# Output projection as three rounded products by half blocks, with the weights' parts reloaded through one buffer

## The reference, cut to what matters

```python
x = x + attention(layernorm(x), Wq, Wk, Wv, Wo, betas)
x = x + ffn(layernorm(x), ...)          # gate: top 4 of 32 experts; shared expert beside it
# attention: 16 heads of 128, segments of 64 tokens, a memory carried from segment to segment
att_dot = softmax(q @ k.T / scale, causal) @ v
att_mem = sigma_q @ mem / (sigma_q @ z)
mem    += sigma_k.T @ (v - sigma_k @ mem / (sigma_k @ z))
att     = beta * att_mem + (1 - beta) * att_dot
out     = att.reshape(Bsz, SEG, H * DV) @ Wo      # 2048 x 256: this product is what changes
```

## Time and profile before

| | |
|---|---|
| time, median of 3 runs | 1655.94 us |
| the profiled execution's own time | 1656.93 us |
| its span | 1655.1 us |
| PE busy | 1626.1 us (98%) |
| PE weight loads | 1421.5 us (86%) |
| DVE busy | 1138.9 us (69%) |
| ACT busy | 884.3 us (53%) |
| POOL busy | 495.9 us (30%) |
| DMA moved | 122.07 MB, 74 GB/s on average |
| PE in the chain that ended last | 92% of the span |

### The profile page before, as it was taken

One profiled execution on the slowest core, in us unless ns is written; L12 is line 12 of the kernel. 1 busy time (PEld: TensorE's weight loads), 2 busy tenths in 40 slices (PEclk: granted clock), 3 DMA queues, 4 the chain that ended last, 5 costly groups with the idle time before them and its releaser, 6 DMA issues.

```text
span 1655.1 us, 42788 instructions
## 1 busy us (share of the span) xinstructions
PE 1626.1 (98%) x17260; PEld 1421.5 (86%) x17260; DVE 1138.9 (69%) x3509; ACT 884.3 (53%) x1955; POOL 495.9 (30%) x438
## 2 busy tenths in 40 slices
PE   8899999999999999999999999999999999999898
PEld 7798999899998999898999989898999989986555
DVE  7865857585775757575776758575876767589544
ACT  6564646465563646365664646364654646462131
POOL 2332323232332313331333313231333323230361
PEclk9999999999999999999999999999999999999999
DMA  6102121211102121312112020312112020327957
GB/s 208 27 21 78 40 73 33 81 33 55 58 29 84 36 72 34 86 34 58 49 35 85 29 78 28 86 34 65 42 41 78 29 78 23 95 90 214 315 103 216
DMA packets 121781, 122.07 MB, mean 74 GB/s; under 512 B 24032, under 2 KB 101296, under 8 KB 121456
## 3 DMA queue, kind: packets, MB, share of 16 engines
q1 hardware_dynamic: 118224, 113.52, 23.0%
q0 software_dynamic: 3328, 5.81, 1.8%
q10 hardware_dynamic: 32, 0.01, 0.0%
HBM read 94.90 MB, written 24.40 MB: 72 GB/s over the span
## 4 chain that ended last, share of the span: by engine, by line
PE 92%; DVE 5%; DMA 1%; issue 1%; ACT 0%; POOL 0%; SPq 0%; DVEq 0%; POOLq 0%; ACTq 0%
PE bank_p L1502 23%; PE bank_v L1620 13%; PE chain_k L1575 6%; PE chain_k L1553 6%; PE bank_a L1510 5%; PE bank_v L1510 5%; PE chain_q L1553 5%; PE bank_s L1523 4%; PE bank_a L1591 3%; PE chain L1553 3%; PE bank_p L1533 3%; PE bank_a L1602 2%; PE bank_v L1602 2%; PE bank_s L1608 2%; PE chain L1575 2%; PE bank_p L1683 1%
## 5 line engine op out<-in xcount | busy, mean ns | idle before, releaser
L595 POOL TENSOR_TENSOR step_place<-step_place 128x512 f32<-128x512 f32 x128 | 166.0, 1297 | 574.9 <-ACT step_place L741 426.3
L763 ACT ACTIVATE step_place<-chain_q,step_place 128x128 f32<-128x128 f32 x384 | 112.8, 367 | 221.1 <-DVE step_place L999 221.1
L1620 PE MATMUL bank_v<-step_place 128*128 128x256 f32 x1024 | 225.3, 381 | 0.7 <-ACT step_place L774 0.7
L1502 PE MATMUL bank_p<-xt_hi,w_hi 128*128 128x256 f32 x1024 | 220.0, 296 | 3.0 <-DVE step_place L987 2.9
L1620 PEld LDWEIGHTS bank_v<-step_place 128*128 128x128 f32 x1024 | 193.2, 190 | 29.2 <-issue 2.6
L1502 PE MATMUL bank_p<-xt_hi,w_lo 128*128 128x256 f32 x1024 | 206.4, 283 | 0.0
L1502 PE MATMUL bank_p<-xt_lo,w_hi 128*128 128x256 f32 x1024 | 206.3, 283 | 0.0
L632 POOL TENSOR_TENSOR step_place<-step_place 128x512 f32<-128x512 f32 x64 | 69.3, 1082 | 435.4 <-DVE step_place L1267 435.4
L1502 PEld LDWEIGHTS bank_p<-xt_hi,w_hi 128*128 128x128 f32 x1024 | 158.3, 191 | 22.4 <-issue 13.8
L987 DVE SCALAR_TENSOR_TENSOR step_place<-step_place,bank_p 128x512 f32<-128x512 f32 x128 | 87.4, 684 | 107.6 <-ACT bank_p L735 107.6
L1502 PEld LDWEIGHTS bank_p<-xt_hi,w_lo 128*128 128x128 f32 x1024 | 159.8, 192 | 0.0
(11 more groups left out here) (225 smaller groups left out, 3959.9 us busy)
## 6 DMA issues: line engine op xcount, KB each, us to landing
step_place<-in_L_attn_Wo_dram SPq DMA_DIRECT2D x128, 256.0 KB, 2.8
step_place<-beta_all SPq DMA_DIRECT2D x64, 256.0 KB, 3.3
expert_place<-in_L_ffn_w_dram SPq DMA_DIRECT2D x24, 512.0 KB, 8.2
expert_sums<-zero SPq DMA_DIRECT2D x16, 272.0 KB, 5.2
expert_rows<-rows_place SPq DMA_DIRECT2D x15, 288.0 KB, 2.3
step_place<-in_L_attn_x_dram SPq DMA_DIRECT2D x16, 256.0 KB, 3.9
turned<-in_L_attn_x_dram SPq DMA_DIRECT2D x16, 256.0 KB, 3.9
x_rows<-rows_place SPq DMA_DIRECT2D x16, 256.0 KB, 2.9
```

The lines of the kernel that those rows point to most:

```text
L595: nc.gpsimd.tensor_tensor(dl[seg][:, :, 0:DK], val[:, seg, :, :], beta_rows[:, :, :], ALU.mult).then_inc(s["vb_ready"], 1)
L763: ins = nc.scalar.activation(to[:, j, :], t[:, at:at + DK], ACT.Copy, scale=rd[:, seg, r:r + 1])
L1502: ins = mm(out, w[:, g, m, c, col], x[:, c, :, :].rearrange("p s t -> p (s t)"), start=i == 0, stop=i == len(parts) - 1)
L1620: ins = mm(bank_v[:, b * D:(b + 1) * D], att[:, b * PIECES + i, :], wo[:, i % WR, :], start=(i == 0 and b == 0), stop=(i == PIECES - 1), s ...
```

## The change

- **Format.** `project_out(k)` now makes three fp32r products for each piece: `att_hi` by both parts of `Wo`, `att_lo` by the rounded part. A call does a quarter of a half block: `WR = 4` pieces, 12 products of 128 by 256. A half is 128 rows: both sequences, both segments, half of each segment's tokens. There are `SLOTS` = 128 calls (before: 16 calls of 64 records).
- **Place.** Two calls a step: `project_out(2n - 5)` between the two halves of the keys' projection, `project_out(2n - 4)` before `project_v(0)`. Call 123 and the four calls of the last half block come after the loop.
- **Parts of `Wo`.** At the start `Wo` is loaded whole, split (`wo_high` on ACT, `wo_low` on POOL), and its parts are stored to DRAM (`store_wo`, SP). In the loop POOL loads 1 MB, the four pieces' parts, before each call (`load_wo(k)`, 128 loads). The buffer `wo` holds exactly those four pieces, so load `k` waits for `wo_used` of call `k - 1`.
- **Parts of the attended block.** ACT makes two copies for each segment instead of one (`att_hi` and a full copy), POOL the difference (`attended_low`), and call `k` of a new half waits for it (`att_split`).
- **Residual.** DVE adds each quarter's result to the input in place (`out_add`, 128 of them, 128 x 256) instead of one 128 x 512 addition a block. Norm, transposes, logits and gate of a block come two steps later or more; the gate of a block ends in the block after.
- **Layout.** A half's 128 partitions are eight runs of 16 rows. Loads of the input, stores of routing rows, the load of the experts' sums and the stores of the output become 8 or 16 DMAs where one or two were.
- **Tail.** The gate of block 15 (of 16) also moves behind the loop; `MID_FIRST, MID_THEN = 4, 7` becomes `MID_THEN = 3`, with no list rounds ahead of the last residual; half of the last output stores go to ACT's queue.
- `sigq` and `sigk` keep three places instead of four, `x_in` shares its place with `turned`, and `pt` its place with `sm`.

```diff
-    WR, WC = 8, 2
-    MID_FIRST, MID_THEN = 4, 7
+    WR, WC = 4, 2
+    QS = PIECES // WR
+    SLOTS = 2 * NBLK * QS
+    MID_THEN = 3
...
+        wo = first.enter_context(nc.sbuf_tensor("wo", [128, WR, 2, D], fp32r))
...
+        def store_wo(c):
+            sp.wait_ge(s["wo_split"], 2 * c + 2)
+            sp.dma_start(scratch["wo"][:, c * WR:(c + 1) * WR, :, :].bitcast(fp32), wo_parts[c % 2].bitcast(fp32)
+                         ).then_inc(s["wo_moved"], 16)
...
+        for k in range(1, NK, 2):
+            n = slice((k - 1) * YB, (k + 1) * YB)
+            for b, g, seg, p in parts():
+                for f in range(2):
+                    sp.dma_start(yt[p, n, f, :], y[b, f, g, seg][:, n, :]).then_inc(acc_arrived[k], 16)
         def store(lo, hi):
-            for b in range(B):
-                sp.dma_start(o[:, lo:hi, b, :], acc[:, lo:hi, b, :]).then_inc(s2["out_stored"], 16)
+            for b, g, seg, p in parts():
+                for f in range(2):
+                    sp.dma_start(o[b, f, g, seg][:, lo:hi, :], acc[p, lo:hi, f, :]
+                                     ).then_inc(s2["out_stored"], 16)
...
+        def attended_low(n):
+            for seg in range(2):
+                pool.wait_ge(s["att_ready"], 2 * n + seg + 1)
+                hi, lo, copy = att_parts(n, seg)
+                nc.gpsimd.tensor_tensor(lo, copy, hi.bitcast(fp32), ALU.subtract
+                                        ).then_inc(s["att_split"], 1)
+        def load_wo(k):
+            if k:
+                pool.wait_ge(s["wo_used"], k)
+            else:
+                pool.wait_ge(s["wo_moved"], 32 * QS)
+            pool.dma_start(wo[:, :, :, :], scratch["wo"][:, k % QS * WR:(k % QS + 1) * WR, :, :]
+                           ).then_inc(wo_arrived, 16)
...
+        attended_low(NT - 1)
+        for k in range(SLOTS - QS, SLOTS):
+            load_wo(k)
+        for n in range(NBLK - 2, NBLK):
+            pool.wait_ge(s["gate_step"], GATE_STEPS * (n + 1))
+            for b, g, seg, p in parts():
+                pool.dma_start(row_parts[b, n, g, seg], xrow[p, :, :]
+                               ).then_inc(s2["last_row_stored"], 16)
...
+                nc.scalar.activation(hi, got, ACT.Copy)
+                nc.scalar.activation(copy, got, ACT.Copy).then_inc(s["att_ready"], 1)
+        def wo_high(c):
+            act.wait_ge(s["wo_moved"], 16 * QS)
+            if c:
+                act.wait_ge(s["wo_split"], 2 * c)
+            if c >= 2:
+                act.wait_ge(s["wo_moved"], 16 * (QS + 2))
...
+        def out_add(k, bank=bank_v):
+            half = k // QS
+            dve.wait_ge(s["wo_used"], k + 1)
...
+            nc.vector.tensor_tensor(rows, rows, bank[:, 0:D], ALU.add).then_inc(s["out_added"], 1)
...
+        def project_out(k, bank=bank_v, start=True, stop=True):
+            half, quarter = divmod(k, QS)
+            g = slice(half % 2, half % 2 + 2)
+            if quarter == 0:
+                pe.wait_ge(s["att_split"], 4 * (half + 1))
+            pe.wait_ge(wo_arrived, 16 * (k + 1))
+            for i in range(WR):
+                a = quarter * WR + i
+                for which, (x, w) in enumerate(((att_hi, 0), (att_hi, 1), (att_lo, 0))):
+                    ins = mm(bank[:, 0:D], x[:, a, g, :].rearrange("p g m -> p (g m)"), wo[:, i, w, :],
+                             start=start and i == 0 and which == 0,
+                             stop=stop and i == WR - 1 and which == 2)
+            ins.then_inc(s["wo_used"], 1)
```

More of the change, by code:

```diff
@@ L386, in body @@
                     load_w(g)
-                for c in range(WR // WC):
-                    load_wo(1, c)
+                store_wo(0)
+                store_wo(1)
                 load_res(0)
+                store_wo(2)
+                store_wo(3)
                 zero_part(0)
@@ L395, in body @@
             else:
-                for c in range(WR // WC, H // WC):
-                    load_wo(blk, c)
-                for c in range(WR // WC):
-                    load_wo(blk + 1, c)
-                store_x1(blk)
+                if not last:
+                    load_x(blk + 1)
+                load_res(2 * blk)
                 zero_part(blk)
             load_betas(n + 2)
-            if not first:
-                store_columns(blk)
             if last:
@@ L416, in body @@
                 load_betas(n + 4)
-            if blk + 2 < NBLK:
-                load_x(blk + 2)
+            if blk > 1 and not last:
+                store_picks(blk - 1)
             if not first:
-                store_routing(blk)
-                if not last:
-                    store_picks(blk)
+                store_columns(blk)
+            load_res(2 * blk + 1)
         def load_x(blk):
@@ L510, in _ @@
         blocks(sp, body)
-        for c in range(WR // WC, H // WC):
-            load_wo(NBLK, c)
         sp.wait_ge(s["v_mm"], 2 * NT)
         sp.wait_ge(s["lists_kept"], 1)
-        sp.wait_ge(s["x1_stored"], 16 * NBLK)
+        sp.wait_ge(s["x1_stored"], 32 * (NBLK - 1))
         for k in range(NK - 1):
@@ L519, in _ @@
         sp.wait_ge(s["att_ready"], 2 * NT)
-        for i in range(6):
+        for i in range(5):
             load_batch(i)
         store_x1(NBLK)
-        for i in range(6, NB):
+        for i in range(5, NB):
             load_batch(i)
@@ L815, in body @@
                 if n:
-                    attended(n - 1, (g - 1) % NG, None if first or g == 0 else blk)
+                    attended(n - 1)
                 if nxt:
@@ L822, in body @@
                     split_hi(g + 2, 2)
-                if g == 1 and not first:
+                if g == 3 and not first:
                     side_x1t(blk)
@@ L967, in x_apply @@
         def x_apply():
-            norm_apply(ln_x, x_in, x_in, "x_normed")
+            norm_apply(ln_x, x_in, [x_in[:, b, :] for b in range(B)], "x_normed")
         def xt_lo_part(count):
@@ L1290, in body @@
                     split_lo(g + 2, 2)
-                if g == 0 and not first:
-                    residual(blk)
-                    x1_stats(blk)
-                    x1_newton(blk, 0, 1)
                 if g == 1 and not last:
@@ L1319, in _ @@
         ins.then_inc(s["lists_kept"], 1)
-        shared_mul(0, 0)
-        dve.wait_ge(s["pickv_ready"], NBLK)
-        dve.wait_ge(s["lists_kept"], 1)
-        for r in range(MID_FIRST):
-            top8(mid_kept, mid, r)
-        residual(NBLK)
+        picks(NBLK - 1)
+        shared_mul(0, 1)
+        dve.wait_ge(s["wo_used"], SLOTS)
+        dve.wait_ge(s["xres_arrived"], 128 * 2 * NBLK)
+        rows = x_half[(2 * NBLK - 1) % 3]
+        nc.vector.tensor_tensor(rows, rows, bank_v[:, 0:D], ALU.add).then_inc(s["out_added"], 1)
         x1_stats(NBLK)
@@ L1547, in head @@
             def head(kind, j):
-                sig = (sigk, sigq)[kind][:, n % 2]
+                sig = (sigk, sigq)[kind][:, place(n, seg)]
                 t, at = chain(kind, j)
@@ L1798, in body @@
                     pe.wait_ge(s["att_ready"], 2 * n)
-                if g == 0 and not first:
-                    project_out(blk, n)
-                if g == 1 and not first:
-                    x1_transposes(blk)
                 if g == 2 and not last:
@@ L1805, in body @@
                     x_transposes()
+                if g == 3 and not first:
+                    x1_transposes(blk)
+                if n >= 2:
+                    project_out(2 * n - 4)
+                if g == 2 and not last:
+                    pe.wait_ge(s["x_turned"], blk + 1)
+                if g == 3 and not first:
+                    pe.wait_ge(s["x1t_ready"], blk)
                 if nxt:
@@ L1811, in body @@
                 if nxt:
-                    if g == 0 and not first:
-                        pe.wait_ge(s["x1_ready"], blk)
-                    if g == 1 and not first:
-                        pe.wait_ge(s["x1t_ready"], blk)
-                    if g == 2 and not last:
-                        pe.wait_ge(s["x_turned"], blk + 1)
+                    if n >= 2:
+                        pe.wait_ge(s["out_added"], 2 * n - 3)
                     project_v(1, gn)
```

448 lines of the change are left out of this document (270 added, 178 removed).

## The result

The changed kernel takes 1716.61 us (median of 4 runs, 1712.29 to 1717.47), the kernel before in the same comparison 1656.26: a ratio of 1.0357, 95% interval 1.0337 to 1.0378. It is 60 us slower. The forecast was slower, by 22 us, with 1716 inside the range. The profiled execution took 1716.84 us with a span of 1715.0, 59.9 above the span of before.

What follows compares the result with a forecast made beforehand. PE was taken to bound the loop, DVE the tail up to the list and SP's stores the end; -30 + 10 + 28 + 14 = +22 us gave 1678 us, with a range of 1655 to 1728.

Steps and rivals of the forecast that it cites:

- The loop, -30: In the loop, 123 calls of 1.44 us replace 15 projections worth 13.81 us each; gain 30 us if PE never waits.
- The 1 MB load, 6 us and 0.6 for the issue: POOL's load into `wo` before each loop call fits windows of 8.5 and 10.9 us, costing nothing.
- Rival 1: Loads of `wo` come too late in the loop, deciding above 7.9 us to landing; 9 us give some 1740; chance 0.18.
- The margin of 1 us for `att_split`: In the loop, POOL's subtractions end near 753, PE asks for them at 754.1 each second step; costed at nothing.
- Rival 3: POOL's subtractions are late for PE's calls in the loop: up to 45 us on the forecast, 1723; chance 0.07.
- The start, +10: Before and in step 0, ACT's roundings wait for POOL's subtractions and two stores: 0 to 15 us, taken as 10.
- The tail up to the list, +28 with the gathers: After the loop, serial loads and calls delay the residual 28 us; list work adds; gathers give 2 back: +28 us.
- L: The end of the loop, 1494.3 before the change; times in the tail are counted from it.
- From the last addition to the list, and the gathers: In the tail, residual to list takes 36 us instead of 34.4, without stalls; less contention at gathers gives 2 back.
- The tail's end, +14: At the end, 72 output stores at 0.4 us each give +13; 32 loads ahead end just in time; taken as +14.
- Rival 2: Whole kernel: 1 MB lands in 4.1 us, tail +16, stores +10, start hidden; sum -4, 1652 us; chance 0.12.
- The forecast's own range: Whole kernel: 1662 to 1697 us around 1678, from the bounds of the three positive terms; chance 0.55.

Runs made afterwards that it cites:

- c3: Changed kernel with one full 32-bit product per piece in place of its three rounded ones, of the rounded parts alone: 1756.5 us.
- d2: Changed kernel with POOL's two subtractions of each step made to wait for the end of the queries' projection on PE: 1734.8 us.
- a3: Changed kernel with a semaphore of its own for ACT's four roundings of Wo, so ACT no longer waits for POOL's subtractions: 1716.8 us.
- a1: Changed kernel with the 32 loads of the experts' sums as 128 partitions by 1 row instead of 16 by 8, output order wrong: 1706.3 us.
- b2: Changed kernel with the experts' sums kept in DRAM in the halves' order and loaded in 4 DMAs of 128 partitions: 1702.2 us.
- b3: b2 with half of the output stores, the second sequence's, issued by POOL instead of SP: 1695.7 us.
- c1: b3 plus a2, ACT's later Wo roundings moved to the first step's end, POOL's subtractions moved too, and another DVE order around the tail: 1654.3 us.
- a2: Changed kernel with the last four calls' parts of Wo in places of their own, loaded by SP at the loop's end, calls back to back: 1694.6 us.

## Why the prediction was right or wrong, point by point

- **The loop, -30.** Right in its mechanism. The call of 1.44 us and c3 bear out its price, the block of 90.45 us stands against 90.3. The gain was 23.0 instead of 30. Fourteen blocks at 0.15 us each are 2; what the five long blocks are over 90.46 adds up to 3.7, of which PE's records show only some waits (0.6 to 1.2 us each); 1.3 are left unassigned. The forecast was made from one block.
- **The 1 MB load, 6 us and 0.6 for the issue.** Taken 1.3 too high for most: 5.3 in the middle, counted from the start of the issue, which the 0.6 had counted twice. Rival 1 (1740) didn't happen, but its mechanism is there: beside SP's bursts five loads took longer than the 7.9 us from which it would decide, up to 9.2. They were too few, and some of them stood ahead of the longer of the two windows.
- **The margin of 1 us for `att_split`.** Right: 1.1 in the trace, 1.5 at every other of these calls. Rival 3 didn't happen; d2 shows that some 1.8 us of delay there would have cost 18.
- **The start, +10.** Right in size (12.6), wrong in part of its mechanism. I had priced the two waits for POOL; a3 shows that they cost nothing by themselves. What costs is the wait for the first two stores, which I had named behind them without a price: PE stands still for 10.0 us behind it. So the size is right in part by luck.
- **The tail up to the list, +28 with the gathers.** The mechanism was right, the size 11.3 too small (37.3 and 2.0). The last addition came at L + 49.0 instead of L + 45. Nearly 2 us of that are my own sum: L + 26 and twice 8.9 and 1.5 make L + 46.8. The rest is not the loads, which came to the calls 126 and 127 9.2 and 7.6 us after issue, 1 less than twice 8.9. It is the calls: the twelve products took 2.7 us instead of 1.44. PE's mean granted clock was 0.71 of full from 1484 to 1533, a mix of its two levels (2.4 and 1.2 GHz), while it idled in the gaps of the load chain.
- **From the last addition to the list, and the gathers.** The list followed 39.7 us later, not 36. I had counted the four more list rounds at 0.9 us, but after the change each of the eight rounds on 64 partitions goes over 384 elements instead of 256 and takes 1.23 us instead of 0.96, some 2 us more than I had added. DVE also waited twice some 1.1 us for products of the shared expert, of which several took 3.75 us instead of 1.88; I had taken out all stalls. PE's mean granted clock between 1533 and 1573 was 0.80, and 0.95 before in the stretch 1512 to 1546. And the 2 us that I gave back for less contention at the gathers did not come, and no row had shown them: the way from list to sums became 2.0 longer.
- **The tail's end, +14.** This is the step that failed: 31.0. I had written that the 32 loads ahead of the stores end just in time, and had timed them by SP's issue (12.8 us). They took until 1691 to land, 38.6 us, as 16 partitions at a time took 115 GB/s: the first store went out 23.0 us after the first load instead of 13.3. a1 and b2 show 10 to 14 us of it. The stores' term was too small as well: 0.535 us each with their waits and 0.48 without (b2) where I took 0.4 from the 345 ns of the fastest and the 470 of the middle, 5 us for the 64; and b3 shows that one queue for all of them costs 6.6.
- **Rival 2 (1652, faster)** needed every lower bound at once; none held. c1 reaches 1654, but by other edits: what it removes are the serial loads, the wait on ACT and the narrow loads, and DVE's order in the tail is a new one.
- **Sum.** -30 + 10 + 28 + 14 = +22 forecast; -23.0 + 12.6 + 37.3 + 2.0 + 31.0 = +59.9 in the trace. Of the 38 us between them 17 are the end, 11 the tail with the gathers, 7 the loop, 3 the start.
- **The range.** That 1716 lies inside 1655 to 1728 is luck: the range was that wide for rivals (3 alone reached to 1723) that did not happen. The forecast's own range ended at 1697, and that range does not follow from the bounds I gave; added up, these run from 1652 to about 1689.

## What to carry to other kernels

A change that is priced by the row of the bounding engine in the loop must be priced again where the loop begins and ends: a buffer with one place, which costs next to nothing in the loop, was 22 us where only four uses are left, some 8 of them because other loads ran beside it. Time a DMA by what it moves through, not only by its issue: the same bytes in the same number of DMAs took 39 us to land in pieces of 16 partitions and 18 in wide ones. And an engine's wait for a store belongs at the end of what others need of it, not in the middle: moving two instructions past the rest of one step gave back 10 us.

## What the runs showed that I had not expected

- Loads and stores of 16 partitions behave differently. Loads were held to 115 GB/s with the DMA engines full; stores (b2) landed in 2.1 us and followed SP's issue, at some 138 GB/s, and a wider, flatter form made the issue dearer (596 ns against 426) and the kernel 10 us slower.
- A second queue for the stores helped less than halving them should: SP's own issue rose from 0.48 to 0.69 us apiece beside POOL's.
- The values of `Wo` that are already rounded, moved by SP as plain 32-bit words (a2), serve PE's rounded products as well as POOL's own loads did; DVE's last addition had no wait left.
